# Shifted-window attention block on one core: the weighed sum of the values with the values standing still, in four column groups

## The reference, cut to what matters

```python
h = roll(layernorm(x) * g1 + b1, (-4, -4))        # over rows and columns of the image
win = window_partition(h, 8)                      # 512 windows of 64 pixels, 64 channels
q, k, v = split(win @ qkv_w + qkv_b)              # 4 heads of 16 channels
attn = einsum('bnhd,bmhd->bhnm', q, k) * 16 ** -0.5 + bias[h, n, m] + mask[window, n, m]
attn = softmax(attn, axis=-1)                     # over m
out = einsum('bhnm,bmhd->bnhd', attn, v)          # the weighed sum
x = x + roll(window_reverse(out @ proj_w + proj_b), (4, 4))
x = x + gelu((layernorm(x) * g2 + b2) @ fc1_w + fc1_b) @ fc2_w + fc2_b
```

## Time and profile before

| | |
|---|---|
| time, median of 3 runs | 516.42 us (514.03 to 518.35) |
| profiled execution, its span | 516.1 us |
| attention stage with the result's divisions | about 54 to 361 us |
| MLP stage | about 361 to 516 us |
| PE busy | 462.7 us (90%) |
| PEld busy | 352.7 us (68%) |
| DVE busy | 388.9 us (75%) |
| ACT busy | 359.0 us (70%) |
| POOL busy | 384.4 us (74%) |

### The profile page before, as it was taken

One profiled execution on the slowest core, in us unless ns is written; L12 is line 12 of the kernel. 1 busy time (PEld: TensorE's weight loads), 2 busy tenths in 40 slices (PEclk: granted clock), 3 DMA queues, 4 the chain that ended last, 5 costly groups with the idle time before them and its releaser, 6 DMA issues.

```text
span 516.1 us, 21507 instructions
## 1 busy us (share of the span) xinstructions
PE 462.7 (90%) x9630; PEld 352.7 (68%) x9630; DVE 388.9 (75%) x549; ACT 359.0 (70%) x501; POOL 384.4 (74%) x376
## 2 busy tenths in 40 slices
PE   0765799999899999999999999998799999999995
PEld 0533587787788788778788778677566666666664
DVE  2865688899779899879899899894467767666752
ACT  0236488878878878778778778775577777777761
POOL 2648959879969979969969978942288888888830
PEclk9998799999999999999999999999999999999999
DMA  8201424411411411411011011000003303311333
GB/s 162 60 1 31 99 47 96 114 34 25 104 38 30 104 39 28 102 34 37 23 29 40 23 25 41 24 23 3 3 3 84 84 12 74 84 46 40 83 83 83
DMA packets 9986, 27.04 MB, mean 52 GB/s; under 512 B 3368, under 2 KB 3368, under 8 KB 7976
## 3 DMA queue, kind: packets, MB, share of 16 engines
q1 hardware_dynamic: 9896, 25.68, 21.1%
HBM read 9.15 MB, written 8.39 MB: 34 GB/s over the span
## 4 chain that ended last, share of the span: by engine, by line
PE 53%; DVE 17%; POOL 16%; ACT 8%; issue 2%; DMA 2%; SPq 0%; ACTq 0%; DVEq 0%
PE work L693 20%; PE outs L693 10%; POOL probs L367 9%; PE trans L693 8%; PE scores L693 6%; DVE negmax L482 5%; DVE probs L476 4%; POOL stat_rstd L333 4%; PE scores L829 3%; PE trans L789 3%; DVE x L517 3%; DMA params<-in_params 2%; POOL xn L344 2%; DVE x L533 2%; ACT qT L605 2%
## 5 line engine op out<-in xcount | busy, mean ns | idle before, releaser
L367 POOL TENSOR_TENSOR probs<-probs,negmax 128x1024 f32<-128x1024 f32 x64 | 123.9, 1937 | 38.4 <-DVE negmax L482 38.4
L333 POOL TENSOR_TENSOR stat_rstd<-stat_var,minus_half 128x8 f32<-128x8 f32 (+1 forms) x62 | 105.0, 1693 | 5.0
L476 DVE TENSOR_TENSOR probs<-scores,bias 128x1024 f32<-128x1024 f32 x64 | 77.9, 1218 | 32.9 <-PE scores L693 32.9
L638 ACT ACTIVATE probs<-probs 128x1024 f32<-128x1024 f32 x64 | 67.7, 1058 | 50.3 <-POOL probs L367 49.8
L338 POOL TENSOR_TENSOR xn<-x,stat_mean 128x256 f32<-128x256 f32 (+1 forms) x91 | 77.2, 867 | 4.1
L482 DVE TENSOR_REDUCE negmax<-probs 128x16 f32<-128x1024 f32 x64 | 78.1, 1220 | 2.2
L693 PEld LDWEIGHTS work<-params,probs 128*64 128x64 f32 x2048 | 62.2, 138 | 23.5 <-DVE x L570 20.5
L693 PE MATMUL scores<-kX,qT 32*64 32x128 f32 x2048 | 71.5, 276 | 7.2 <-DVE probs L476 4.6
L693 PE MATMUL outs<-vX,probsT 128*64 128x34 f32 x2048 | 72.9, 226 | 5.1 <-ACT probsT L643 4.1
L693 PEld LDWEIGHTS outs<-vX,probsT 128*64 128x64 f32 x2048 | 66.0, 139 | 16.4 <-issue 9.5
L789 PEld LDWEIGHTS trans<-ident,probs 128*128 128x128 f32 x512 | 56.2, 142 | 26.4 <-issue 14.2
(11 more groups left out here) (64 smaller groups left out, 691.7 us busy)
## 6 DMA issues: line engine op xcount, KB each, us to landing
kX<-kT SPq DMA_DIRECT2D x124, 64.0 KB, 2.0
x<-in_x SPq DMA_DIRECT2D x32, 224.0 KB
out<-x SPq DMA_DIRECT2D x28, 224.0 KB
x<-in_x SPq DMA_DIRECT2D x32, 32.0 KB
out<-x SPq DMA_DIRECT2D x28, 32.0 KB
out<-x SPq DMA_DIRECT2D x16, 56.0 KB
params<-in_params SPq DMA_DIRECT2D x1, 741.5 KB, 12.3
out<-x SPq DMA_DIRECT2D x16, 8.0 KB
```

The costliest lines, as they stand in the source:

```text
L333: nc.gpsimd.tensor_tensor(stat_rstd[:, cols], stat_var[:, cols], minus_half[:, cols], ALU.pow).then_inc(ln_rstd, pieces)
L367: nc.gpsimd.tensor_tensor(e, e, top, ALU.add).then_inc(shifted, 1)
L476: nc.vector.tensor_tensor(e[:, :].rearrange("q (u a m) -> q a u m", u=2, a=2), scores[:, :].rearrange("q (a u m) -> q a u m", a=2, u=2), b ...
L638: nc.scalar.activation(probs[n % 4][:, :], probs[n % 4][:, :], ACT.Exp)\
```

## The change

The roles in the weighed sum are swapped: the values stand still, and the transposed probabilities move. For each part, 16 products load 32 columns of values (two heads, with the other half of the rows zero) into one of four column groups of the array, and 64 columns of probabilities move past them. The result comes out already transposed, with channels on the partitions. Since there is no column of ones in `vX` any more, four more products with a 32-column tile `head_ones` (ones in the place of the values) give the row sums, each moving 256 columns: every channel of a head gets its own copy of its row sum, in the second half of the bank. `divide` takes the reciprocal of these 256 columns and multiplies the 256 columns of the result by them, straight into `oT`. The order of heads and windows in the scores, the bias and `vX` is changed to suit: the values are copied by four ACT instructions of 64 x 256 instead of two of 64 x 512, and the bias is built by six additions instead of three. `transpose_o` and `copy_oT` are gone, and both banks of `outs` now serve the weighed sum in turn: `weigh(n)` waits for `divide(n - 2)`.

```diff
-VW = 2 * (HD + 1)
+VW = 2 * HD
-        outs, outsT = outs2[:, 0:BANK], outs2[:, BANK:2 * BANK]
+        outs = [outs2[:, 0:BANK], outs2[:, BANK:2 * BANK]]
-        vX = [sb(f"vX{i}", 32, VW) for i in range(2)]
+        vX = [sb(f"vX{i}", 2, 8, 2, VW) for i in range(2)]
+        head_ones = sb("head_ones", VW)
-        inverse = [sb(f"inverse{i}", 16) for i in range(2)]
+        inverse = [sb(f"inverse{i}", 2 * P) for i in range(2)]
...
             def divide(n):
-                o = outs[:, 0:16 * (HD + 1)].rearrange("q (t d) -> q t d", d=HD + 1)
+                g, step = divmod(n, STEPS)
+                bank = outs[n % 2]
                 dve.wait_ge(outs_ready, n + 1)
-                nc.vector.reciprocal(inverse[n % 2][:, :], o[:, :, HD]).then_inc(inverse_ready, 1)
+                nc.vector.reciprocal(inverse[n % 2][:, :], bank[:, 2 * P:4 * P]).then_inc(inverse_ready, 1)
                 dve.wait_ge(inverse_ready, n + 1)
-                nc.vector.tensor_tensor(o_rows[n % 2][:, :].rearrange("q (t d) -> q t d", d=HD),
-                                        o[:, :, 0:HD],
-                                        inverse[n % 2][:, :].unsqueeze(2).to_broadcast([P, 16, HD]),
-                                        ALU.mult).then_inc(outs_taken, 1)
+                dst = oT[g % 2][:, :].rearrange("q (a i r) -> q i a r", i=2 * STEPS, r=WIN)
+                nc.vector.tensor_tensor(
+                    dst[:, 2 * step:2 * step + 2],
+                    bank[:, 0:2 * P].rearrange("q (i a r) -> q i a r", i=2, r=WIN),
+                    inverse[n % 2][:, :].rearrange("q (i a r) -> q i a r", i=2, r=WIN),
+                    ALU.mult).then_inc(outs_taken, 1)
...
                 elif kind == "V":
                     for p in range(2):
-                        half = slice(N * p, N * (p + 1))
-                        src = work2[half, :].rearrange("q (w a) -> q w a", w=2)[:, :, 0:4 * C]
-                        dst = vX[par][half, :, (HD + 1) * p:(HD + 1) * p + HD]
-                        done = nc.scalar.activation(
-                            dst.rearrange("q (w a) d -> q w a d", w=2),
-                            src.rearrange("q w (a d) -> q w a d", d=HD), ACT.Copy)
+                        for odd in range(2):
+                            done = nc.scalar.activation(
+                                vX[par][N * odd:N * (odd + 1), p, :, :, HD * odd:HD * (odd + 1)],
+                                src[N * p:N * (p + 1), odd], ACT.Copy)
...
-            def copy_oT(n):
-                act.wait_ge(oT_ready, n + 1)
...
             def weigh(n):
                 image, k = divmod(n, 2)
+                bank = outs[n % 2]
                 if k == 0:
                     copied("V", image // GI, image % GI)
                 pe.wait_ge(trans_copied, n + 1)
-                if n:
-                    pe.wait_ge(outs_taken, n)
+                if n >= 2:
+                    pe.wait_ge(outs_taken, n - 1)
                 else:
                     pe.wait_ge(y_bias_made, 1)
+                    pe.wait_ge(zeroed, 2)
+                tiles = [(slice(32 * (2 * p + a), 32 * (2 * p + a + 1)), p, a) for p in range(2) for a in range(2)]
                 for u in range(2):
-                    for h in range(HEADS):
-                        for w in range(2):
-                            at = (u * HEADS + h) * P + w * N
-                            row = (w * 4 + 2 * k + u) * HEADS + h
-                            out = outs[w * N:(w + 1) * N, u * HEADS * VW:(u + 1) * HEADS * VW]\
-                                .rearrange("q (p h d) -> q p h d", p=2, h=HEADS)[:, :, h]
-                            done = mm(out, probsT[n % 2][:, at:at + N], vX[image % 2][:, row, :])
+                    for w in range(2):
+                        for rows, p, a in tiles:
+                            at = (4 * u + 2 * a + p) * P + w * N
+                            mm(bank[rows, u * P + w * N:][:, 0:N],
+                               vX[image % 2][:, p, 4 * w + 2 * k + u, a, :],
+                               probsT[n % 2][:, at:at + N])
+                for rows, p, a in tiles:
+                    both = probsT[n % 2][:, :].rearrange("q (u t m) -> q t u m", u=2, m=P)
+                    done = mm(bank[rows, 2 * P:4 * P].rearrange("q (u m) -> q u m", u=2),
+                              head_ones[:, :], both[:, 2 * a + p])
                 done.then_inc(outs_ready, 1)
-
-            def transpose_o(n):
-                pe.wait_ge(outs_taken, n + 1)
...
```

More of the change, by code:

```diff
@@ L422, in _ @@
             for t in range(2):
-                done = nc.vector.memset(vX[t][:, :, :], 0.0)
-            done.then_inc(vX_zeroed, 1)
+                nc.vector.memset(vX[t][:, :, :, :, :], 0.0)
+            nc.vector.memset(head_ones[:, :], 0.0).then_inc(vX_zeroed, 1)
             dve.wait_ge(vX_zeroed, 1)
[L426 to L429, removed]
+            for odd in range(2):
+                done = nc.vector.memset(head_ones[N * odd:N * (odd + 1), HD * odd:HD * (odd + 1)], 1.0)
             done.then_inc(zeroed, 1)
@@ L452, in _ @@
             dve.wait_ge(y_bias_summed, 1)
-            nc.vector.tensor_tensor(y_bias[:, :], outs[:, 0:C], bproj[:, :], ALU.add)\
+            nc.vector.tensor_tensor(y_bias[:, :], outs[0][:, 0:C], bproj[:, :], ALU.add)\
               .then_inc(y_bias_made, 1)
@@ L458, in _ @@
                     continue
[L460 to L463, removed]
+                m = mask[:, j * P:(j + 1) * P].rearrange("q (p m) -> q p m", p=2).unsqueeze(2)\
+                    .to_broadcast([P, 2, 2, N])
                 for at in ((0, 1), (2,))[j]:
-                    nc.vector.tensor_tensor(
-                        bias[:, at, :].rearrange("q (h p m) -> q h p m", h=HEADS, p=2), r, m,
-                        ALU.add).then_inc(bias_made, 1)
+                    for a in range(2):
+                        r = rpb[:, a * P:(a + 1) * P].rearrange("q (o m) -> q o m", o=2).unsqueeze(1)\
+                            .to_broadcast([P, 2, 2, N])
+                        done = nc.vector.tensor_tensor(
+                            bias[:, at, a * 2 * P:(a + 1) * 2 * P].rearrange("q (p o m) -> q p o m", p=2, o=2),
+                            r, m, ALU.add)
+                    done.then_inc(bias_made, 1)
             dve.wait_ge(bias_made, 3)
@@ L607, in take @@
                 elif kind == "V":
+                    src = work2[:, :].rearrange("q (a z) -> q a z", a=8)[:, :, 0:C]\
+                        .rearrange("q a (b o d) -> q o a b d", b=2, o=2)
                     for p in range(2):
-                        half = slice(N * p, N * (p + 1))
-                        src = work2[half, :].rearrange("q (w a) -> q w a", w=2)[:, :, 0:4 * C]
-                        dst = vX[par][half, :, (HD + 1) * p:(HD + 1) * p + HD]
-                        done = nc.scalar.activation(
-                            dst.rearrange("q (w a) d -> q w a d", w=2),
-                            src.rearrange("q w (a d) -> q w a d", d=HD), ACT.Copy)
+                        for odd in range(2):
+                            done = nc.scalar.activation(
+                                vX[par][N * odd:N * (odd + 1), p, :, :, HD * odd:HD * (odd + 1)],
+                                src[N * p:N * (p + 1), odd], ACT.Copy)
                     done.then_inc(v_copied, 1)
@@ L728, in fill @@
                                 rows = slice(C * w, C * (w + 1))
-                                done = mm(work[w][N * p:N * (p + 1), wi * C:(wi + 1) * C],
+                                done = mm(work[w][N * p:N * (p + 1), wi * 2 * C:wi * 2 * C + C],
                                           xT[of % 2][rows, at:at + N], wqkv[rows, 2, C * w:C * (w + 1)])
@@ L733, in fill @@
                     if i == 0:
[L734 removed]
+                        pe.wait_ge(outs_taken, STEPS * (of + 1))
                     for c in range(WIN):
@@ L778, in score @@
                                 rows = slice(32 * (2 * w + hh), 32 * (2 * w + hh + 1))
-                                out = scores[w * N:(w + 1) * N, hh * BANK + u * 256:][:, 0:256]\
-                                    .rearrange("q (h p m) -> q p h m", h=2, p=2)[:, p]
+                                to = hh * BANK + (2 * u + p) * P
+                                out = scores[w * N:(w + 1) * N, to:to + P].rearrange("q (o m) -> q o m", o=2)
                                 done = mm(out, qT[two][rows, at:at + N], kX[two][rows, :, at:at + N])
@@ L856, in _ @@
             pe.wait_ge(trans_copied, PAIRS)
-            pe.wait_ge(oT_copied, PAIRS)
+            pe.wait_ge(outs_taken, PAIRS)
             copied("Y", GROUPS - 1, 1)
```

21 lines of the change are left out of this document (1 added, 20 removed).

## The result

The changed kernel takes 568.42 us, median of 4 runs (567.21 to 571.16), against 516.51 us before: the ratio is 1.102, with a 95% interval from 1.097 to 1.107. It is slower, by 52 us; 578 was forecast, within 560 to 612.

A forecast was written before the change was run, and what follows sets the result against it. TensorE was taken to set the pace, with VectorE second and little idle time. From 516.1 us: 97.3 added for the reciprocals, 34.2 off as covered, 1.0 off at the end, giving 578 us; range 560 to 612.

The forecast's parts named there:

- The likeliest case: Attention stage: the wide reciprocal on VectorE outgrows its idle time and lengthens the stage; 578 us in all, chance 0.62.
- The price of the reciprocal: VectorE, each part: 256 columns take 1.77 us instead of 0.25, the middle of 1.57 and 1.97 us.
- Rival (b): VectorE's reciprocal: eight passes a column, 8.3 ns a column and 2.24 us each; 609 us in all, chance 0.16.
- Rival (a): VectorE's reciprocal runs at one column a cycle and TensorE stays the bound; 511 us, between 503 and 520, chance 0.14.
- The added work and its cover: VectorE, attention stage: 97.3 us more reciprocal work, of which 34.2 us is covered by waits that vanish.
- The point of decision: VectorE hides a reciprocal below some 0.78 us (2.2 ns a column): 34 us of cover, 0.53 us more a part.
- 1.21 us for the weighed sum: TensorE, each part: 0.69 us for eight rounds of four tiles plus 0.52 us for the ones, 0.13 us more.
- rival (c): TensorE's weighed sum: four column groups with 128 rows don't run together; 586 us in all, chance 0.06.
- the main case: Attention stage: VectorE's work grows by more, so TensorE's 6 us saving is worth nothing except about 1.0 us at the end.
- The MLP stage: The stage after attention was to keep its 155 us.
- Rival (d): TensorE's granted clock falls to half for long, its blocks double and the time passes 650 us; chance 0.02.
- 14 us less: ScalarE: 24.8 us less for the result's copy, 10.5 us more for the values' copies; no effect on the time.

The follow-up runs named there:

- a_recip16: The changed kernel with the reciprocal cut from 256 to 16 columns (most of the result not divided rightly): 513.84 us, ratio 0.996 to the kernel before.
- a_no_ones: The changed kernel without the four products with ones, except for the first two parts: 570.94 us, ratio 1.102 to the kernel before.
- b_recip64: The kernel before with only the reciprocal widened, from 16 to 64 columns: 520.32 us, ratio 1.0075.

## Why the prediction was right

**The likeliest case came.** VectorE's reciprocal is the cause, shown from both sides: narrow in the changed kernel (the loss goes) and wide in the kernel before (it comes). The time lies 1.7% under the forecast.

**The price of the reciprocal** was taken as the middle of two estimates from rows, 1.77 us; it is 1748 ns. The excess of 71 ns over a plain instruction of 16 columns does go with the columns. A column costs 6.25 ns, with 147 ns fixed, between the 5.5 and 7.2 that bounded it. It is six times the 1.04 ns of a plain column. Rival (b), eight passes a column, would be 8.3 ns and 2.24 us, and is out. The Trainium skill ("VectorE: DVE Perf Modes", "First, the fixed hardware budget") gives the reciprocal a repeat count of 8; a column that costs six times a plain one agrees with its sense, but read as eight times a plain column the count is not what the rows give. Rival (a), one column a cycle, is out.

**The added work and its cover.** Forecast were 97.3 us more of work less 34.2 covered, less 1.0 at the end: 62.1. From 361.39 to 410.84 the stage grew by 49.4. VectorE's busy time grew by 349.7 - 260.7 = 89.0 us, 8.3 less than forecast: 1.2 of that is the reciprocal's price, 3.5 lie in the additions of the bias to x (L517 before, 29.5 us; L519 now, 26.0), and the rest I did not follow. Its idle time fell from 46.7 to 7.1 us, by 39.6 and not by 34.2 + 1.0 = 35.2: the waits for scores gave 26.1 us (forecast 25.0), those for the weighed sums 5.8 (3.0), those for Y the 6.2 forecast, and the rest, the end of the stage included, 1.5 (1.0). So the cover was counted nearly right, and the larger part of the 12.7 us, 8.3, is the term of the added work. That 578 was only 9 us too high against the profiled execution is partly luck: 12.7 too much in this stage, 3.7 too little in the next.

The point of decision that I gave for rival (a), 0.78 us a reciprocal, takes cover as a store. In the kernel before, with its one bank, that holds roughly: 0.55 us a reciprocal lengthened the stage by 0.4 us, and 0.95 us by 10.1, where 44.9 - 34.2 = 10.7 would have been the count. In the changed kernel no width between 16 and 256 was run.

**TensorE.** I forecast 1.21 us for the weighed sum; it takes 1.02. Four tiles with 128 rows do run together (rival (c) is out). The eight rounds take 0.47 us and not 0.69, because I had taken their price from a block with its start and the change of shape behind it in it; the ones take 0.55 against 0.52. So TensorE saves 16 us in a_recip16 and not 6. That the saving is worth nothing in the main case is shown by a_no_ones. Rival (a) would have come near in the stage: it had 7.4 us off the kernel before less a few for ScalarE's copies, and a_recip16 has 5.8 off, since 10 of the 16 us went into waiting for them. That its time is 514 and not 511 lies, in its profiled execution, in the MLP stage.

**The MLP stage** "should keep its 155 us": wrong, it took 158.4. Rival (d), the clock, had been put aside since no gap of TensorE would pass some 1.5 us. Its waits went up to 2.4 and 2.8 us, and the clock did fall, never for long: in six short stretches between 57 and 365 us, where TensorE was not the bound (a_no_ones, with more of them, was no slower), and from 412.5 us, where it was, for 3.6 us in all.

**ScalarE**: 14 us less were forecast. By its rows it is 24.8 less for the copy of the result and 48.4 - 39.0 = 9.4 more for the values; the busy time, in which overlapping rows count once, fell from 359.0 to 352.2 us. No effect on the time was forecast, and none is seen.

## What to carry to other kernels

Before swapping the roles in a product, look at the shape in which its by-products come out: here 16 row sums a partition became 256, and an operation at six times the price of a plain column was made 16 times as wide on the second busiest engine. Price what is widened by its slope, and get the slope out of the one size at hand by subtracting what a plain instruction of that size takes. Count an engine's cover from the waits that the added work can fill, and check it stage by stage: in the whole time, a lower clock in a stage that nobody touched (2 to 4 us here) looks like cover that failed. And an instruction that is moved to an engine with room can cost three times its length (22.5 us of copies, some 68 us) if it waits there ahead of what everyone else needs; where it stands in the order can matter more than how long it is.

## What the runs showed of the hardware

- The reciprocal of VectorE from PSUM: 247, 548, 948 and 1748 ns for 16, 64, 128 and 256 columns, 6.25 ns a column and 147 ns fixed.
- Four tiles of 128 rows x 32 columns run together: rounds of 64 moving columns start 0.056 to 0.06 us apart (0.47 us for eight). Two tiles of 64 columns before, with 34 moving columns, took 0.066 us a round with the change of shape behind them (16 rounds in 1.06 us).
- TensorE's granted clock fell to its lower level at 412.5 us in the changed kernel, after idle times of 1.85 us and, in part, 1.34 us around a block of 1.16 us. It fell in b_recip64 too, where the first idle time was 0.56 us, and stayed up in the kernel before with 0.57. It stayed up in both kernels with extra matmuls there. At the lower level a Y block of 1.16 us took 1.98.
